# A graph-attention kernel on one core: the score's bias becomes a 17th term of each head, and one VectorE pass sums it

## The chip, the cores and the metric

One core of one Trainium2 chip runs the whole program. The metric is device time in microseconds (us) of one execution, as the median of several. The core has five engines that run side by side and wait for each other through semaphores: TensorE (PE in the profile; its weight loads stand apart as PEld), VectorE (DVE), ScalarE (ACT), GpSimd (POOL) and SyncE (SP), which here only issues DMAs.

## What is computed

The reference is a two-layer graph network over 12,500 nodes and 200,000 edges with vectors of 128 numbers. The change is inside the second layer, an attention over edges with 8 heads of 16 numbers each:

```
scores = einsum('ehd,ehd->eh', q[row], k[col]) / sqrt(16)
scores = scores + edge_emb @ eb_w.T + eb_b          # the bias: 8 numbers per edge
exp_scores = exp(scores - segment_max(scores, row)[row])
attn = exp_scores / segment_sum(exp_scores, row)[row]
out = segment_sum(attn * v[col], row) @ out_w.T + out_b
```

For every edge and head a score is the sum of 16 products of q and k, plus one bias. The division by 4 is already in q, and the 8 biases of every edge were worked out earlier in the kernel.

## The kernel before

The kernel is a sequence of phases with a barrier between them. An earlier phase writes one row per edge into `kv_sorted` in HBM, sorted by the node that collects: 128 numbers of k, then 8 biases (`BIAS_AT` = 128), then a small number `LO_AT` that says which of 128 nodes of a tile the edge belongs to, with v behind them. The score phase reads the first part of these rows (`PART` = 144 numbers).

The score phase works on tiles of 128 edges (an edge per partition). Four tiles are a **group** (`GROUP` = 4), four groups are a **turn** (`GROUPS` = 4), and there are 105 turns, so 420 groups. `by_turns` writes turns 0 and 1 out with fixed numbers and runs nearly all others in a loop of two turns a pass, so an even turn is followed directly by an odd one, and behind an odd one stands the branch back. In the lines below g is the group's number, and j (0 to 3) its place in the turn. What each engine does, in its own order:

- SyncE (`load`, L1873 to L1877) issues one DMA per group, 288 KB into `k_rows`, which holds two turns. It waits until the group two turns earlier has been scored (`scored`) and its `LO_AT` column kept (`lows_kept`).
- TensorE, in `turn`: four matmuls `spread_keys(g + 1)` (L1958), that spread the edges' `LO_AT` over the columns of a bank; then a load of four node numbers from SBUF into registers (`loaded`); then a wait for `hot_ready` and the matmuls of L1991, four of fp32, which the trace records as eight, that pick each edge's q row: bank (2 + j % 2). Behind group 1 of the turn come the three small matmuls of `compare` (L1969 to L1971), behind group 2 the transpose `move_scores` (L1965), and behind group 3 `move_breaks` (L1979), which waits for `flagged`.
- VectorE, in `turn`: `one_hots(g + 1)` (L2019) compares the spread numbers with the partition's own and writes the weights `hot_t`; then `score` of the group before. `score` is two instructions: a TENSOR_REDUCE (L2025) sums the 16 products of each head into `part_scores`, and a TENSOR_TENSOR (L2029) adds the bias from `k_rows` and writes `scores`. At j = 2 `flag` (L2035) follows, on whose `flagged` `move_breaks` waits.
- ScalarE: `lows` (L1889) keeps the `LO_AT` column of a group some two groups ahead, `keep_q(g)` (L1895) copies the q rows from PSUM to `q_sb`; once a turn `keep_scores` (L1899) and `keep_breaks` (L1903).
- GpSimd: one TENSOR_TENSOR (L1946) per group multiplies `q_sb` and the k part of `k_rows` into `qk`, a buffer of two groups; it waits for `q_kept` and for `reduced` of two groups before.

`hot_t`, `q_sb`, `qk`, `part_scores` and the banks are all doubled. All numbers of this path are fp32.

Of the kernel before, what the change touches and what calls it, by code (L numbers as in the profile page):

```python
# [6 lines left out]
ALU, ACT, AX = mybir.AluOpType, mybir.ActivationFunctionType, mybir.AxisListType  # L7

P = 128
N_NODES, N_EDGES, D = 12500, 200000, 128  # L10
HEADS = 8
HEAD_DIM = D // HEADS
# [25 lines left out]
BIAS_AT, LO_AT = D, D + HEADS  # L38
# [15 lines left out]
def need(eng, sem, value):  # L54

    if isinstance(value, int) and value <= 0:
        return
    eng.wait_ge(sem, value)
# [31 lines left out]
def gnn(nc, x, src, dst, attr, w1, b1, w2, b2, gamma, beta, bn_mean, bn_var,  # L90
# [14 lines left out]
    with whole:  # L105
# [98 lines left out]
        with ExitStack() as ph:  # L204
            sem = ph.enter_context(phase_semaphores(nc))
            tmp = lambda n, s, d=F32: ph.enter_context(nc.sbuf_tensor(n, s, d))
# [1389 lines left out]
        with ExitStack() as ph:  # L1596
            own = ph.enter_context(phase_semaphores(nc))
            sem = lambda n: own(f"qkv_{n}")
            tmp = lambda n, s, d=F32: ph.enter_context(nc.sbuf_tensor(f"qkv_{n}", s, d))
# [98 lines left out]
        GROUP = 4  # L1698
        GROUPS = TURN // GROUP


        GROUP = 4
        GROUPS = TURN // GROUP
        with ExitStack() as ph:
            own = ph.enter_context(phase_semaphores(nc))
            sem = lambda n: own(f"expand_{n}")
            tmp = lambda n, s, d=F32: ph.enter_context(nc.sbuf_tensor(f"expand_{n}", s, d))
            spread, hot_ready, made, joined, cleared = (sem(n) for n in ("spread", "hot_ready", "made", "joined", "cleared"))
# [131 lines left out]
        def static_turn(i, *turns):  # L1840

            return isinstance(i, int) and i in turns
# [3 lines left out]
        with ExitStack() as ph:  # L1846
            own = ph.enter_context(phase_semaphores(nc))
            sem = lambda n: own(f"score_{n}")
            tmp = lambda n, s, d=F32: ph.enter_context(nc.sbuf_tensor(f"score_{n}", s, d))
            PIECES = 7  # L1850
            lows_kept, q_in, nodes_placed, shapes, shapes_cleared = (
                sem(n) for n in ("lows_kept", "q_in", "nodes_placed", "shapes", "shapes_cleared"))
            spread, hot_ready, q_ready, q_kept, product, reduced, scored = (
                sem(n) for n in ("spread", "hot_ready", "q_ready", "q_kept", "product", "reduced", "scored"))
            moved, kept_s, differs, flagged, b_moved, kept_b = (
                sem(n) for n in ("moved", "kept_s", "differs", "flagged", "b_moved", "kept_b"))
            k_in = [[sem(f"k_in{b}{j}") for j in range(GROUPS)] for b in range(2)]
            k_rows = tmp("k_rows", [P, 2, GROUPS, GROUP, PART])
            hot_t = tmp("hot_t", [P, 2, GROUP * P])
            q_sb, qk = tmp("q_sb", [P, 2, GROUP * D]), tmp("qk", [P, 2, GROUP * D])  # L1860
            part_scores = tmp("part_scores", [P, 2, GROUP * HEADS])
            scores = tmp("scores", [P, 2, TURN, HEADS])
            flags = tmp("flags", [P, TURN, HEADS], BF16)
            slot_step, tile_step, break_diag = (tmp(n, [P, P], BF16) for n in ("slot_step", "tile_step", "break_diag"))
# [3 lines left out]
            @block.sync  # L1868
            def _(sp):
                q_tiles = q_table.rearrange("(n p) d -> p n d", p=P)  # L1870

                def load(i, b, m):
                    for j in range(GROUPS):  # L1873
                        need(sp, scored, (i - 2) * GROUPS + j + 1)
                        need(sp, lows_kept, (i - 2) * GROUPS + j + 1)
                        rows = kv_turns[:, bass.ds(i, 1), j * GROUP:(j + 1) * GROUP, 0:PART]
                        sp.dma_start(k_rows[:, b, j, :, :], rows.rearrange("p a c f -> p (a c) f")).then_inc(k_in[b][j], 16)  # L1877
                    if static_turn(i, 0):
                        for n in range(PIECES):
                            some = slice(n * NT // PIECES, (n + 1) * NT // PIECES)  # L1880
                            sp.dma_start(nodes[:, some, :], q_tiles[:, some, :]).then_inc(q_in, 16)

                by_turns(sp, load)

            @block.scalar
            def _(act):
                def lows(i, b, m, j):
                    act.wait_ge(k_in[b][j], m * 16 + 16)
                    act.copy(lo_turns[:, bass.ds(i * TURN + TURN + j * GROUP, GROUP)],  # L1889
                             k_rows[:, b, j, :, LO_AT:LO_AT + 1].rearrange("p m a -> p (m a)")).then_inc(lows_kept, 1)  # L1890

                def keep_q(g, b):
                    act.wait_ge(q_ready, g + 1)
                    need(act, product, g - 1)
                    act.copy(q_sb[:, b, :], bank[2 + b][:, :]).then_inc(q_kept, 1)  # L1895

                def keep_scores(i):
                    act.wait_ge(moved, i + 1)
                    act.copy(scores_t[:, bass.ds(i * P, P)], bank[6][:, 0:P]).then_inc(kept_s, 1)  # L1899

                def keep_breaks(i, count):
                    act.wait_ge(b_moved, count)
                    act.copy(breaks[:, bass.ds(i * P, P)], bank[5][:, 0:P]).then_inc(kept_b, 1)  # L1903

                def turn(i, b, m):
                    for j in range(GROUPS):
                        if j < 2:
                            lows(i, b, m, j + 2)
                        elif not static_turn(i, S_TURNS - 1):
                            lows(i + 1, 1 - b, m + b, j - 2)  # L1910
                        keep_q(i * GROUPS + j, j % 2)
                        if j == 3 and not static_turn(i, 0):
                            keep_scores(i - 1)
                        if j == 3 and not static_turn(i, 0, 1):
                            keep_breaks(i - 1, i - 1)

                for j in range(2):
                    lows(0, 0, 0, j)
                by_turns(act, turn)
                keep_scores(S_TURNS - 1)  # L1920
                keep_breaks(S_TURNS - 1, S_TURNS - 1)
                keep_breaks(0, S_TURNS)

            @block.gpsimd
            def _(pool):
                g = nc.gpsimd
                for shape in (slot_step, tile_step, break_diag):
                    g.memset(shape[:, :], 0.0).then_inc(shapes_cleared, 1)
                pool.wait_ge(shapes_cleared, 3)
                g.affine_select(out=slot_step[:, :], in_=slot_step[:, :], compare_op=ALU.not_equal, fill=1.0, base=0,  # L1930
                                pattern=[[-1, P]], channel_multiplier=1).then_inc(shapes_cleared, 1)
                g.affine_select(out=tile_step[:, :], in_=tile_step[:, :], compare_op=ALU.not_equal, fill=-1.0, base=-(P - 1),
                                pattern=[[-1, P]], channel_multiplier=1).then_inc(shapes, 1)
                g.affine_select(out=break_diag[:, :], in_=break_diag[:, :], compare_op=ALU.not_equal, fill=BREAK, base=0,
                                pattern=[[-1, P]], channel_multiplier=1).then_inc(shapes, 1)
                pool.wait_ge(shapes_cleared, 4)
                g.affine_select(out=slot_step[:, :], in_=slot_step[:, :], compare_op=ALU.not_equal, fill=-1.0, base=-1,
                                pattern=[[1, P]], channel_multiplier=-1).then_inc(shapes, 1)

                def turn(i, b, m):  # L1940
                    for j in range(GROUPS):
                        n = i * GROUPS + j
                        pool.wait_ge(k_in[b][j], m * 16 + 16)
                        pool.wait_ge(q_kept, n + 1)
                        need(pool, reduced, n - 1)
                        g.tensor_tensor(qk[:, j % 2, :].rearrange("p (m d) -> p m d", d=D),  # L1946
                                        q_sb[:, j % 2, :].rearrange("p (m d) -> p m d", d=D),
                                        k_rows[:, b, j, :, 0:D], ALU.mult).then_inc(product, 1)

                by_turns(pool, turn)  # L1950

# [61 lines left out]
            def _(dve):  # L2013
                v = nc.vector
# [6 lines left out]
                def score(i, b, j):  # L2021
                    g = i * GROUPS + j
                    dve.wait_ge(product, g + 1)
                    need(dve, scored, g - 1)
                    v.tensor_reduce(part_scores[:, j % 2, :], qk[:, j % 2, :].rearrange("p (m d) -> p m d", d=HEAD_DIM), AX.X, ALU.add).then_inc(reduced, 1)  # L2025
                    dve.wait_ge(reduced, g + 1)
                    if j == 0:
                        need(dve, moved, i - 1)
                    v.tensor_tensor(scores[:, b, j * GROUP:(j + 1) * GROUP, :], k_rows[:, b, j, :, BIAS_AT:BIAS_AT + HEADS],  # L2029
                                    part_scores[:, j % 2, :].rearrange("p (m h) -> p m h", h=HEADS), ALU.add).then_inc(scored, 1)  # L2030

                def flag(count):
                    dve.wait_ge(differs, count)
# [366 lines left out]
```

## Time and profile before

| what | value |
|---|---|
| median of 3 runs | 9340.34 us |
| lowest and highest of them | 9325.51 and 9343.74 us |
| the profiled execution's own time | 9325.89 us |
| its span, first to last instruction | 9324.3 us |
| mean granted TensorE clock over the span | 0.790 |

The profile comes from one execution. A time of the profile is in us from the first instruction. The granted clock is a share of 2.4 GHz. The busy shares of the 40 slices are averages over phases that are bound by different things; the score phase is slices 32 to 36, about 7253 to 8267 us.

### The profile page before, as it was taken

The numbers are of one execution on the slowest core, as the hardware profiler recorded it, in microseconds if no ns is written. First come the engines' busy times: TensorE is split into PE (matmuls) and PEld (weight loads), VectorE is DVE, ScalarE is ACT, GpSimd is POOL, SyncE is SP. The second block draws the span as 40 slices with busy tenths as digits, with TensorE's granted clock in tenths as the row PEclk, the third lists the DMA queues.
The fourth block names the chain that finished last, engine by engine and source line by source line (L and its number), as shares of the span: only waits on it lengthen the run. The fifth ranks groups of instructions, "written<-read, shape, count | busy, mean of one in ns | idle before, by whom it ended". The sixth has DMA issues, their size and how long they took to land. (4 is left out here: it accounts for less than half of the span.)

```text
span 9324.3 us, 229377 instructions
## 1 busy us (share of the span) xinstructions
PE 6847.9 (73%) x40334; PEld 5733.4 (61%) x40335; DVE 6225.0 (67%) x23634; ACT 3314.6 (36%) x10654; POOL 5973.0 (64%) x6648
## 2 busy tenths in 40 slices
PE   7789999999868888888884656666666577735774
PEld 5578888888747777776773444444444466625663
DVE  8755555555547777777776655555555688897777
ACT  7533333333324444444441100000000233316884
POOL 4467776666656666666667577777777455526665
PEclk9876666666668888888885888888888899978997
DMA  1043333333342211111112333333333544414553
GB/s 45 8 113 104 105 104 104 102 102 102 89 124 53 52 51 51 51 50 50 48 49 62 110 113 113 113 113 113 113 113 113 140 126 125 126 51 131 151 153 93
DMA packets 1057790, 868.52 MB, mean 93 GB/s; under 512 B 214825, under 2 KB 950425, under 8 KB 1057737
## 3 DMA queue, kind: packets, MB, share of 16 engines
q0 software_dynamic: 179664, 437.87, 15.4%
q1 hardware_dynamic: 643032, 319.49, 13.1%
q10 hardware_dynamic: 235040, 110.58, 4.2%
q8 instruction: 18, 0.29, 0.0%
q14 instruction: 36, 0.29, 0.0%
HBM read 578.04 MB, written 287.84 MB: 93 GB/s over the span
## 5 line engine op out<-in xcount | busy, mean ns | idle before, releaser
L1420 POOL DMA_INDIRECT spmm_rows<-h_table,spmm_index_ring x3136 | 2968.3, 947 | 1472.4 <-issue 886.2
L1491 PE MATMUL bank<-spmm_rows,spmm_hot 128*128 x6660 | 1951.2, 395 | 117.8 <-SPq L1397 71.1
L1765 POOL DMA_INDIRECT kv_sorted<-expand_payload,expand_where_ring x1568 | 1519.1, 969 | 500.6 <-issue 418.4
L1465 DVE TENSOR_TENSOR region_ab<-region_ab,bank 128x128 f32 x3330 | 956.1, 287 | 1213.9 <-PE bank L1491 1165.9
L1786 PE MATMUL bank<-region_ab,expand_hot_t 128*128 x3336 | 1107.5, 490 | 773.4 <-DVE expand_hot_t L1802 773.1
L1491 PEld LDWEIGHTS bank<-spmm_rows,spmm_hot 128*128 128x128 f32 x6660 | 1421.9, 265 | 214.0 <-issue 184.3
L1818 DVE SCALAR_TENSOR_TENSOR expand_payload<-expand_payload,region_c,bank 128x256 f32 x1668 | 801.5, 481 | 893.7 <-SPq L1730 406.2
L1786 PEld LDWEIGHTS bank<-region_ab,expand_hot_t 128*128 128x128 f32 x3336 | 770.8, 242 | 975.2 <-issue 849.0
L1449 DVE TENSOR_SCALAR spmm_hot<-iota_bf,lo_slots 128x128 f32<-128x128 bf16 x3334 | 1001.3, 300 | 20.0 <-issue 18.7
L1946 POOL TENSOR_TENSOR score_qk<-score_q_sb,score_k_rows 128x512 f32<-128x512 f32 x420 | 532.3, 1267 | 477.4 <-ACT score_q_sb L1895 464.2
L456 ACT ACTIVATE spmm_beside_sign<-iota_half,region_c 128x128 bf16<-128x128 bf16 x1568 | 521.8, 392 | 828.8 <-DVE spmm_beside_bias_sb L545 681.0
L689 PE MATMUL bank<-spmm_beside_next_slot,spmm_beside_lo_t 128*128 128x98 f32 x3136 | 807.3, 346 | 0.3
L1991 PE MATMUL bank<-region_ab,score_hot_t 128*128 x3360 | 521.3, 302 | 211.1 <-ACT score_q_sb L1895 98.4
L2275 PE MATMUL bank<-mix_mixed,mix_hot 128*128 128x136 f32 x3360 | 506.8, 310 | 211.1 <-DVE region_ab L2239 195.0
L724 ACT COPY spmm_beside_next_slot<-bank 128x98 f32<-128x98 f32 x1568 | 379.7, 242 | 744.5 <-PE bank L683 729.2
L2176 POOL TENSOR_TENSOR mix_mixed<-mix_mixed 128x512 f32<-128x512 f32 x420 | 453.4, 1100 | 268.2 <-ACT mix_mixed L2191 178.3
L2275 PEld LDWEIGHTS bank<-mix_mixed,mix_hot 128*128 128x128 f32 x3360 | 466.6, 208 | 249.9 <-DVE region_ab L2239 229.8
L689 PEld LDWEIGHTS bank<-spmm_beside_next_slot,spmm_beside_lo_t 128*128 128x128 f32 x3136 | 580.9, 231 | 49.0
L1991 PEld LDWEIGHTS bank<-region_ab,score_hot_t 128*128 128x128 f32 x3360 | 443.6, 206 | 261.7 <-issue 261.4
L683 PE MATMUL bank<-spmm_beside_hot_hi,spmm_beside_hot_lo 128*128 128x98 bf16 x1568 | 357.7, 228 | 328.2 <-issue 328.2
L1751 ACT COPY expand_where_ring<-region_c 128x8 int32 x196 | 38.7, 197 | 1541.5 <-SPq L1730 1531.1
L469 PE MATMUL bank<-spmm_beside_sign,spmm_beside_hot_hi 128*98 128x128 bf16 x1568 | 453.4, 289 | 162.7 <-ACT spmm_beside_sign L456 76.0
(350 smaller groups left out, 13957.6 us busy)
## 6 DMA issues: line engine op xcount, KB each, us to landing
score_k_rows<-kv_sorted SPq DMA_DIRECT2D x420, 288.0 KB
mix_mixed<-kv_sorted SPq DMA_DIRECT2D x420, 256.0 KB
spmm_beside_attr_sb<-in_edge_attr_dram ACTq DMA_DIRECT2D x390, 256.0 KB
spmm_rows<-h_table,spmm_index_ring POOLq DMA_INDIRECT x3136
kv_sorted<-expand_payload,expand_where_ring POOLq DMA_INDIRECT x1568
kv_sorted<-spmm_beside_blank SPq DMA_DIRECT2D x1, 15232.0 KB
kv_sorted<-spmm_beside_blank SPq DMA_DIRECT2D x98, 136.0 KB
h_table<-region_ab SPq DMA_DIRECT2D x28, 448.0 KB, 3.0
```

The source lines that it names most:

```text
L456: nc.scalar.activation(self.sign[:, slot, :], iota_half[:, :], ACT.Sign, bias=self.lo[:, bass.ds(c, 1)], scale=-1.0).then_inc(self.signs_r ...
L689: t.matmul(self.found_in[k % 2][:, 0:NT], self.lo_t[:, k // 2 % self.PAIRS, at], self.next_slot[:, k % 2, :], start=True, stop=False)
L1420: nc.gpsimd.indirect_dma_start(rows[:, h * HALF + k, :], None, table, bass.IndirectOffsetOnAxis(ap=index_ring[:, h, k:k + 1], axis=0)).the ...
L1449: nc.vector.tensor_scalar(hot[:, k % HOTS, :], iota_bf[:, :], lo_slots[:, bass.ds(t, 1)], None, ALU.is_equal).then_inc(row_hot_ready, 1)
L1465: nc.vector.tensor_tensor(here, here, sum_bank[k % 2][:, 0:D], ALU.add).then_inc(added, 1)
L1491: nc.tensor.matmul(sum_bank[k % 2][:, 0:D], hot[:, k % HOTS, :], tile_of(rows, place[k % HALF]), start=True, stop=True).then_inc(summed, 1)
L1765: nc.gpsimd.indirect_dma_start(kv_sorted, bass.IndirectOffsetOnAxis(ap=where_ring[:, h, k:k + 1], axis=0), payload[:, h * HALF + k, 0:ROW] ...
L1786: nc.tensor.matmul(into, hot_t[:, j % 2, m * P:(m + 1) * P], tile_of(kv_nodes, node[m]), start=True, stop=True).then_inc(made, 1)
L1818: v.scalar_tensor_tensor(here, here, same_window[:, bass.ds(t, 1)], made_here, ALU.mult, ALU.add).then_inc(joined, 1)
L1946: g.tensor_tensor(qk[:, j % 2, :].rearrange("p (m d) -> p m d", d=D), q_sb[:, j % 2, :].rearrange("p (m d) -> p m d", d=D), k_rows[:, b, j ...
L1991: last = nc.tensor.matmul(bank[2 + j % 2][:, n * D:(n + 1) * D], hot_t[:, j % 2, n * P:(n + 1) * P], tile_of(nodes, node[n]), start=True, ...
L2275: last = nc.tensor.matmul(bank[k % RING][:, stream * W:(stream + 1) * W], hot[:, b, c, :], mixed[:, b, c, :], start=True, stop=True)
```

## The change

GpSimd's product writes into a new tile `terms`, in which every head has 17 places in a row, the first 16 for the products. ScalarE gets one more copy per group, `place_bias`, which puts the 8 biases of each edge into the 17th places. VectorE's reduce sums 17 numbers and writes `scores` directly; the TENSOR_TENSOR, `part_scores` and the semaphore `reduced` go. `terms` takes the bytes that `qk` and `part_scores` had together (4,352 per partition). GpSimd waits for `scored` where it waited for `reduced`. SyncE's loads wait for `product` and `bias_placed` where they waited for `scored` and `lows_kept`.

```diff
-            q_sb, qk = tmp("q_sb", [P, 2, GROUP * D]), tmp("qk", [P, 2, GROUP * D])
-            part_scores = tmp("part_scores", [P, 2, GROUP * HEADS])
+            TERMS = HEAD_DIM + 1
+            q_sb, terms = tmp("q_sb", [P, 2, GROUP * D]), tmp("terms", [P, 2, GROUP, HEADS, TERMS])
...
-                        need(sp, scored, (i - 2) * GROUPS + j + 1)
-                        need(sp, lows_kept, (i - 2) * GROUPS + j + 1)
+                        need(sp, product, (i - 2) * GROUPS + j + 1)
+                        need(sp, bias_placed, (i - 2) * GROUPS + j + 1)
...
+                def place_bias(i, b, j):
+                    need(act, scored, i * GROUPS + j - 1)
+                    act.copy(terms[:, j % 2, :, :, HEAD_DIM:TERMS].rearrange("p m h a -> p m (h a)"),
+                             k_rows[:, b, j, :, BIAS_AT:BIAS_AT + HEADS]).then_inc(bias_placed, 1)
...
                         keep_q(i * GROUPS + j, j % 2)
+                        place_bias(i, b, j)
...
-                        need(pool, reduced, n - 1)
-                        g.tensor_tensor(qk[:, j % 2, :].rearrange("p (m d) -> p m d", d=D),
-                                        q_sb[:, j % 2, :].rearrange("p (m d) -> p m d", d=D),
-                                        k_rows[:, b, j, :, 0:D], ALU.mult).then_inc(product, 1)
+                        need(pool, scored, n - 1)
+                        g.tensor_tensor(terms[:, j % 2, :, :, 0:HEAD_DIM],
+                                        q_sb[:, j % 2, :].rearrange("p (m h d) -> p m h d", h=HEADS, d=HEAD_DIM),
+                                        k_rows[:, b, j, :, 0:D].rearrange("p m (h d) -> p m h d", d=HEAD_DIM), ALU.mult).then_inc(product, 1)
...
                     dve.wait_ge(product, g + 1)
-                    need(dve, scored, g - 1)
-                    v.tensor_reduce(part_scores[:, j % 2, :], qk[:, j % 2, :].rearrange("p (m d) -> p m d", d=HEAD_DIM), AX.X, ALU.add).then_inc(reduced, 1)
-                    dve.wait_ge(reduced, g + 1)
+                    dve.wait_ge(bias_placed, g + 1)
                     if j == 0:
                         need(dve, moved, i - 1)
-                    v.tensor_tensor(scores[:, b, j * GROUP:(j + 1) * GROUP, :], k_rows[:, b, j, :, BIAS_AT:BIAS_AT + HEADS],
-                                    part_scores[:, j % 2, :].rearrange("p (m h) -> p m h", h=HEADS), ALU.add).then_inc(scored, 1)
+                    v.tensor_reduce(scores[:, b, j * GROUP:(j + 1) * GROUP, :].rearrange("p m h -> p (m h)"),
+                                    terms[:, j % 2, :, :, :].rearrange("p m h d -> p (m h) d"), AX.X, ALU.add).then_inc(scored, 1)
```

## Rows read from the trace of the kernel before

**Rows 1.** TensorE's busy tenths and granted clock in 40 slices of the span

```profile
PE   7789999999868888888884656666666577735774
...
PEclk9876666666668888888885888888888899978997
```

**Rows 2.** Groups of instructions in the score phase: busy us, mean ns | idle before, releaser

```profile
L1946 POOL TENSOR_TENSOR score_qk<-score_q_sb,score_k_rows 128x512 f32<-128x512 f32 x420 | 532.3, 1267 | 477.4 <-ACT score_q_sb L1895 464.2 <-DVE score_part_scores L2025 13.1
...
L2019 DVE TENSOR_SCALAR score_hot_t<-bank,iota_p 128x512 f32<-128x512 f32 x420 | 311.7, 742 | 52.2 <-PE bank L1958 48.5
L2025 DVE TENSOR_REDUCE score_part_scores<-score_qk 128x32 f32<-128x512 f32 x420 | 283.4, 675 | 94.3 <-POOL score_qk L1946 94.3
L2029 DVE TENSOR_TENSOR score_scores<-score_k_rows,score_part_scores 128x32 f32<-128x32 f32 x420 | 276.2, 658 | 14.4
```

**Rows 3.** The tile part_scores: durations in ns, min/median/max, of its two instructions

```profile
L2025 DVE TENSOR_REDUCE score_part_scores<-score_qk x420: 668/672/689, 7287.2 to 8265.0; 128x32 f32<-128x512 f32 x140
L2029 DVE TENSOR_TENSOR score_scores<-score_k_rows,score_part_scores x420: 191/781/1272, 7287.9 to 8265.7; 128x32 f32<-128x32 f32 x140
```

**Rows 4.** Line L1991 alone in one stretch: us, PE busy (count), PEld, PEclk, DMA share, GB/s

```profile
7300.00:8256.00 956.00, 506.02 (x3264) 430.49 (x3264) 0.95 0.50 126
```

**Rows 5.** VectorE and GpSimd in order of time: start us, us, instruction

```profile
7541.02 0.94 DVE L2029 TENSOR_TENSOR score_scores<-score_k_rows,score_part_scores 128x32 f32<-128x32 f32 x1
7541.89 0.28 DVE L2035 TENSOR_SCALAR score_flags<-bank 128x128 bf16<-128x128 f32 x1
...
7540.65 1.26 POOL L1946 TENSOR_TENSOR score_qk<-score_q_sb,score_k_rows 128x512 f32<-128x512 f32 x1 [0.97 <-ACT score_q_sb L1895]
```

**Rows 6.** TensorE in order of time, an odd turn (from 7534.67) between two even ones

```profile
7532.19 1.15 PE L1991 MATMUL bank<-region_ab,score_hot_t 128*128 x8 [0.92 <-DVE score_hot_t L2019]
...
7534.67 1.16 PE L1991 MATMUL bank<-region_ab,score_hot_t 128*128 x8 [0.59 <-issue]
...
7536.56 1.16 PE L1991 MATMUL bank<-region_ab,score_hot_t 128*128 x8 [0.51 <-ACT score_q_sb L1895]
...
7538.80 1.15 PE L1991 MATMUL bank<-region_ab,score_hot_t 128*128 x8 [0.51 <-ACT score_q_sb L1895]
...
7540.83 1.15 PE L1991 MATMUL bank<-region_ab,score_hot_t 128*128 x8 [0.54 <-ACT score_q_sb L1895]
7542.22 0.23 PE L1979 MATMUL bank<-score_break_diag,score_flags 128*128 128x128 bf16 x1 [0.23 <-DVE score_flags L2035]
...
7544.16 1.15 PE L1991 MATMUL bank<-region_ab,score_hot_t 128*128 x8 [0.60 <-issue]
...
7546.06 1.15 PE L1991 MATMUL bank<-region_ab,score_hot_t 128*128 x8 [0.52 <-ACT score_q_sb L1895]
...
7548.43 1.15 PE L1991 MATMUL bank<-region_ab,score_hot_t 128*128 x8 [0.51 <-issue]
...
7550.52 1.16 PE L1991 MATMUL bank<-region_ab,score_hot_t 128*128 x8 [0.52 <-ACT score_q_sb L1895]
...
7553.39 1.15 PE L1991 MATMUL bank<-region_ab,score_hot_t 128*128 x8 [0.59 <-issue]
```

**Rows 7.** TensorE in order of time, an odd turn that starts at half clock

```profile
7703.30 2.07 PE L1991 MATMUL bank<-region_ab,score_hot_t 128*128 x8 [0.62 <-issue]
...
7705.59 1.52 PE L1991 MATMUL bank<-region_ab,score_hot_t 128*128 x8
...
7707.45 1.16 PE L1991 MATMUL bank<-region_ab,score_hot_t 128*128 x8
...
7709.94 1.15 PE L1991 MATMUL bank<-region_ab,score_hot_t 128*128 x8 [1.00 <-DVE score_hot_t L2019]
...
7712.82 0.93 PE L1991 MATMUL bank<-region_ab,score_hot_t 128*128 x6 [0.64 <-issue]
```

**Rows 8.** Groups of instructions of the whole program, as in group 2

```profile
L1754 ACT COPY expand_payload<-expand_bias_ring 128x64 f32<-128x64 f32 x196 | 47.9, 244 | 351.2 <-DMA expand_bias_ring<-bias_tab 351.2
...
L2082 POOL TENSOR_TENSOR region_ab<-region_ab 128x3360 f32<-128x3360 f32 x1 | 17.7, 17726 | 139.9 <-DVE region_ab L2118 139.9
```

More of the change, by code:

```diff
@@ L1852, in gnn @@
                 sem(n) for n in ("lows_kept", "q_in", "nodes_placed", "shapes", "shapes_cleared"))
-            spread, hot_ready, q_ready, q_kept, product, reduced, scored = (
-                sem(n) for n in ("spread", "hot_ready", "q_ready", "q_kept", "product", "reduced", "scored"))
+            spread, hot_ready, q_ready, q_kept, product, bias_placed, scored = (
+                sem(n) for n in ("spread", "hot_ready", "q_ready", "q_kept", "product", "bias_placed", "scored"))
             moved, kept_s, differs, flagged, b_moved, kept_b = (
```

## The prediction

> **What bounds the kernel now.** I read the page first, for TensorE's two rows of slices [rows 1]: the change touches only the score phase, and the rest I leave as it is. Then the groups of that phase [rows 2], to see which engine has the work; the tile's own view [rows 3], to see whether a duration is a price or a wait; one line in one stretch [rows 4], for the period; and last the engines in order of time [rows 5 to 7], because only there can be seen who waits for whom.
>
> The period: between 7300 and 8256 us there are 3,264 records of L1991, 32 to a turn, so 102 turns in 956 us: 9.373 us a turn, 2.34 a group [rows 4]. Per group VectorE is busy 742 + 675 + 658 ns [rows 2], four times 2.075, and 0.28 for the flag [rows 5]: 8.58 us of a turn's 9.37. It looks like the bound, and GpSimd with 1.267 of 2.34 does not.
>
> The third of the three durations isn't a price. The TENSOR_TENSOR of L2029 handles 32 numbers per partition, yet takes between 191 and 1272 ns, while the reduce before it, on 512 numbers, always takes 668 to 689 [rows 3]. The rows in time show what it is: L2029 runs from 7541.02 to 7541.96, GpSimd's product from 7540.65 to 7541.91 [rows 5]. It ends some 50 ns behind the product, and the longest one is as long as a whole product. I read it as an instruction with two SBUF inputs that can't go on while GpSimd's product runs; 191 ns is its price alone.
>
> Is VectorE then the bound? TensorE must be asked, since it closes each period. I take the distance from one start of L1991 to the next. An odd turn goes 1.89, 2.24, 2.03, 3.33 us (from 7534.67 to 7544.16); the next even one 1.90, 2.37, 2.09, 2.87 (to 7553.39) [rows 6]. In the short three nobody waits for VectorE: TensorE has four spreading matmuls, a register load of half a microsecond (the idle time of 0.51 to 0.60 before L1991, whatever name stands behind it), and 1.15 us of matmuls. In the fourth there is a real wait, L1979 on the flag (0.23 us idle, then the queue starts up again), since the flag at 7541.89 stood behind the stretched L2029 [rows 5, 6]. So the two engines are nearly equal, and **VectorE costs TensorE only the lateness at the end of a turn**, not its whole surplus.
>
> How long is the fourth distance with no wait? An even turn shows it: 7532.19 to 7534.67 is 2.48, with no idle time named at L1979. An odd turn shows 7709.94 to 7712.82, 2.88: the loop's branch is in that one [rows 6, 7].
>
> **The change, part by part.**
>
> *Removed: L2029 and the waits beside it*, 420 instructions, 276 us of VectorE [rows 2]. *Grown: the reduce*, from 512 to 544 numbers. Row L2025 gives 1.31 ns a number with its fixed part inside [rows 3], so at most 0.042 us more; at the least nothing. I take 0.035. VectorE's turn falls from 8.58 to 4 x (0.742 + 0.675 + 0.035) + 0.28 = 6.1 us, far below TensorE's.
>
> *Added: ScalarE's copy*, 32 numbers. The nearest row copies 64 from SBUF to scattered places in 0.244 us [rows 8], so between nothing and 0.244; I take 0.22, or 0.9 us a turn. It stands behind the copy of q, for which GpSimd waits, so it delays no product of its own group, and the reduce needs it only when the product of 1.267 us is done. Its wait for `scored` of two groups earlier could hold ScalarE, and with it `lows` and the next `keep_q`. That score is queued on VectorE directly behind the one-hots that L1991 of this very group needed, so it is over some 0.7 us after L1991 began, while ScalarE gets to the copy only after L1991's 1.15 us and its own 0.6. Cost: nothing; without this cover ScalarE would pay the difference per group.
>
> *Moved: where the product writes.* The inputs are the same, but the output goes in runs of 16 with a gap of one. No row of before has such an output on GpSimd. From below 1.267 us [rows 2]; nothing makes it cheaper. From above, the dearest product per number in the trace, 17.7 us for 3,360 numbers or 5.28 ns, makes 2.70 us for 512 [rows 8]. That one ran alongside VectorE's own subtraction; the shape is nearest to L1946 itself, so I take 1.27. Up to about 2.2 us per group, TensorE's period, it stays hidden.
>
> *Moved: SyncE's waits.* The loads wait for the product and the bias copy, both earlier than the score. ScalarE keeps the lows of a group before its bias, so dropping that wait changes nothing. DMA is busy 0.50 of the stretch and the loads run a turn ahead [rows 4]; worth nothing in either direction. GpSimd now waits for the whole score of two groups before, which is the reduce it always waited for.
>
> *What is late next.* The product of a group starts 1.85 us behind its L1991 (7538.80 to 7540.65) [rows 5, 6] and ends at 3.1; the reduce of 0.71 ends at about 3.9. The flag, queued behind the score of group 1, is then done 4.2 us after group 1's L1991 began. L1979 asks for it after two more distances and 1.15 us of matmuls, 2.24 + 2.03 + 1.15 = 5.4 at the earliest. The one-hots of a group start at the latest 2.0 us after the L1991 two groups before theirs (3.9 less a distance of 1.89), end at 2.8, and are wanted at 4.1. Both have over a microsecond to spare, so all waits of TensorE for VectorE should go, and TensorE's own issue and matmuls set the turn.
>
> *The sum.* Without waits an even turn is 1.90 + 2.37 + 2.09 + 2.48 = 8.84 us, an odd one 1.89 + 2.24 + 2.03 + 2.88 = 9.04, mean 8.94. Against 9.373 that is 0.433 a turn, 102 turns: 44 us. Some distances could still hold a little waiting that I can't see; if even turns issued as quickly as odd ones (2.24 and 2.03 for 2.37 and 2.09) it would be 0.53 a turn, 54 us. The first turns and the phase's tail lose one stretched L2029 or two: 1 us. So **45 us less**. In terms of the profiled execution 9325.9 becomes 9281; that one stands at the low end of the runs shown, and the median of 9340.3 is what is compared, so it becomes 9295.
>
> **Rivals.**
>
> *The stretch passes on, or had no hold on the end: no change, 9340.* If whatever GpSimd holds falls on the next VectorE instruction, the reduce would now take up to 1.27 us and the flag be as late as before. Against it: reduces that overlapped products throughout never exceeded 689 ns [rows 3]. The Trainium skill ("VectorE: DVE Perf Modes", The TRN2 errata) gives an fp32 tensor_tensor (N + 151)/0.96 ns, which is 191 for N = 32. By that rule VectorE's turn would be 6.7 us, never late, and the change would be worth nothing; the trace agrees with the smallest duration only, and has a mean of 658. Both together 0.10.
>
> *Half the gain: 9318.* One of the margins above is eaten, by the added semaphore waits or by a product that costs 1.5 us or more, and the flag is late in one of the two turns of a pass: 51 times 0.4 to 0.5 us less than forecast. Nothing shows it, only estimates exclude it. 0.13.
>
> *TensorE's clock falls: slower.* The granted clock is 0.95 in this stretch [rows 4], and 0.6 in slices in which TensorE is busy 9 tenths and more, 0.8 in those with 8 [rows 1]. If a fuller TensorE brought it to 1.2 GHz (half clock) more often, L1991 takes 2.07 us instead of 1.15 and the distance behind it 2.29 instead of 1.89 [rows 7]: 0.40 a group, 4 a turn. It eats 45 us once a quarter to 30% of the 408 groups go at 1.2 GHz; now about a tenth does. At a share of one half the time is 9295 + 0.4 x 408 x 0.40 = 9360. Against it: the half-clock stretches stand right behind the turn's long last distance, 3.33 or 2.87, where TensorE had idled longest, and now that distance shrinks; and the half-clock turn's first two distances add to 4.15, against 4.13 at 2.4 GHz [rows 6, 7], since the register load overlaps the slower matmuls. The Trainium skill ("TensorE: Matmul & The Clock Gate", Part 1) has it that idling lowers the clock and activity releases it; by that rule the half-clock stretches would rather vanish and the sum be 9293. 0.05.
>
> *GpSimd becomes the bound: slower.* At the upper price of 2.70 us a group the phase takes 420 x (2.70 - 2.34) = 151 us more, 9491; it turns against the change above 2.34. 0.02.
>
> **How the numbers follow.** The forecast 9295 has 0.70, its own range 9280 to 9308: the two sums of 44 and 54 us and the runs' spread. The rivals have 0.10, 0.13, 0.05 and 0.02. The range of eight in ten runs from 9275 to 9325, which takes in the half gain. Faster by over 0.2% means below 9321.7, about what a measurement of this kernel can tell from no change: the forecast and two thirds of the half gain, 0.79. Within 0.2%: the no-change rival and the rest, 0.14. Slower: 0.07.
>
> **What the changed profile would show.** VectorE's reduce at 0.70 to 0.71 us, never longer, and no idle time at L1979 on the flag nor at L1991 on the one-hots. Distances of L1991 of about 1.9, 2.3, 2.05 and then 2.5 or 2.9. The product at 1.27, ScalarE's new copy at 0.20 to 0.24 with no idle time before it. The turn at 8.9 us. It would be wrong if reduces stretch, if the product is over 2.2 us, if the clock falls under 0.85 in this stretch, or if one of the three short distances grows.

## The result, and the profile after

The changed kernel takes 9243.0 us (median of 4 runs, 9235.72 to 9259.46) against 9341.32 us before (median of 4, 9325.51 to 9343.74): ratio 0.9901, 95% interval 0.9883 to 0.9918, so 77 to 109 us less. The forecast was 9295, 45 us less, with a range from 9275. The direction was right and the gain was twice what I worked out.

The profiled execution took 9239.79 us, 86.1 less than that of before. The page of the changed kernel, its head and TensorE's two rows of slices:

```profile
span 9238.2 us, 229276 instructions
...
PE   7789999999958888888886556666666577736773
...
PEclk9876666666668888888886787887888899978997
```

The phases before the change are where they were: the first L1991 (now L1997) starts at 7283.03 us, and at 7283.02 before. The groups of the score phase, which answer to [rows 2] (busy us, mean ns, idle before and releaser):

```profile
L1952 POOL TENSOR_TENSOR score_terms<-score_q_sb,score_k_rows 128x512 f32<-128x512 f32 x420 | 533.7, 1271 | 389.7 <-ACT score_q_sb L1900 369.6 <-DVE score_scores L2033 19.9 <-issue 0.2
...
L2025 DVE TENSOR_SCALAR score_hot_t<-bank,iota_p 128x512 f32<-128x512 f32 x420 | 312.8, 745 | 35.1 <-PE bank L1964 26.8
L2033 DVE TENSOR_REDUCE score_scores<-score_terms 128x32 f32<-128x544 f32 x420 | 302.4, 720 | 275.0 <-POOL score_terms L1952 274.8
...
L1894 ACT COPY score_terms<-score_k_rows 128x32 f32<-128x32 f32 x420 | 104.2, 248 | 0.0
```

The product with its gaps costs 1.271 us (1.267 before), ScalarE's copy 0.248 with no idle time ahead of it, the reduce 0.720 at the mean. VectorE now idles 275 us waiting for products, so it has slack. L1997 alone in the same 102 turns as in [rows 4] (us, PE busy, PEld busy, granted clock, DMA share, GB/s):

```profile
7297.77:8170.59 872.82, 470.56 (x3264) 394.88 (x3264) 1.00 0.53 137
```

8.557 us a turn in place of 9.373: 0.816 less, 83.2 us in 102 turns. The first two turns give 2.3 us more, the last turn and the tail about 1. Where in the turn does it come from? TensorE in order of time, an even turn and the odd one behind it, which answer to [rows 6]:

```profile
7555.16 1.15 PE L1997 MATMUL bank<-region_ab,score_hot_t 128*128 x8 [0.60 <-issue]
...
7557.05 1.15 PE L1997 MATMUL bank<-region_ab,score_hot_t 128*128 x8 [0.51 <-ACT score_q_sb L1900]
...
7559.41 1.15 PE L1997 MATMUL bank<-region_ab,score_hot_t 128*128 x8 [0.52 <-issue]
...
7561.51 1.15 PE L1997 MATMUL bank<-region_ab,score_hot_t 128*128 x8 [0.51 <-ACT score_q_sb L1900]
7562.50 0.22 PE L1985 MATMUL bank<-score_break_diag,score_flags 128*128 128x128 bf16 x1
7562.56 0.45 PE L1964 MATMUL bank<-ident_bf,lo_turns 128*128 128x128 bf16 x4
7563.63 1.15 PE L1997 MATMUL bank<-region_ab,score_hot_t 128*128 x8 [0.62 <-ACT score_q_sb L1900]
...
7565.51 1.15 PE L1997 MATMUL bank<-region_ab,score_hot_t 128*128 x8 [0.50 <-ACT score_q_sb L1900]
...
7567.76 1.15 PE L1997 MATMUL bank<-region_ab,score_hot_t 128*128 x8 [0.54 <-ACT score_q_sb L1900]
...
7569.75 1.15 PE L1997 MATMUL bank<-region_ab,score_hot_t 128*128 x8 [0.50 <-ACT score_q_sb L1900]
```

The reader is to see three distances that did not move at all, 1.89, 2.36, 2.10 and 1.88, 2.25, 1.99, as forecast, and a fourth of 2.12 us in the even turn (7561.51 to 7563.63). In the odd one it is 2.52 (the next start is 7572.27). I had forecast 2.48 and 2.88. Nearly the whole miss is 0.36 us in one place of each turn.

What was wrong with 2.48 can be seen in the two kernels' rows around the flag's matmul. VectorE before: the flag of the even turn that I had taken as free of a wait, that of the next even turn, and that of the odd turn that I had taken as free (its last L1991 starts at 7709.94 [rows 7]):

```profile
7532.77 0.28 DVE L2035 TENSOR_SCALAR score_flags<-bank 128x128 bf16<-128x128 f32 x1
...
7551.52 0.28 DVE L2035 TENSOR_SCALAR score_flags<-bank 128x128 bf16<-128x128 f32 x1
...
7710.54 0.28 DVE L2035 TENSOR_SCALAR score_flags<-bank 128x128 bf16<-128x128 f32 x1
```

and TensorE before, at the first of them:

```profile
7533.18 0.22 PE L1979 MATMUL bank<-score_break_diag,score_flags 128*128 128x128 bf16 x1
7533.46 0.61 PE L1958 MATMUL bank<-ident_bf,lo_turns 128*128 128x128 bf16 x4
```

The flag ended at 7533.05, while the last L1991's matmuls, begun at 7532.19 [rows 6], ran until 7533.34. So no matmul idled, and yet the next of the four spreading matmuls (`spread_keys`) came 0.28 us behind L1979, where in the changed kernel it comes 0.06 behind (7562.50 to 7562.56), and its four matmuls are done in 0.45 instead of 0.61 us. The hypothesis that the runs had to test: TensorE's issue reaches the wait for the flag long before the array does, and while it stands there it prepares nothing of what follows.

The trace has records of TensorE's sequencer too, its waits and register instructions, which the rows shown leave out. In all 102 turns of both kernels the instruction just ahead of the flag's wait is over 0.48 to 0.51 us after the turn's last big matmul group began. In the kernel before, the sequencer's next record begins 0.05 us behind the end of the flag, in all 102 turns. In the changed kernel it begins 0.13 us after the start of the one ahead of it, again in all 102. So in the kernel before the sequencer stood at the flag from about 0.49 us on, while the matmuls ran to 1.15.

### The profile page after: what moved, and what is told of

It reads as the page before. It is cut to its first block and busy times, and to the rows that moved or that the text cites. A ratio compares the mean times of both kernels' runs of the same rounds, so it can differ in the third digit from the quotient of the medians.

```text
span 9238.2 us, 229276 instructions
## 1 busy us (share of the span) xinstructions
PE 6786.1 (73%) x40334; PEld 5668.8 (61%) x40335; DVE 5985.6 (65%) x23214; ACT 3366.2 (36%) x11074; POOL 5983.4 (65%) x6648
## 5 line engine op out<-in xcount | busy, mean ns | idle before, releaser
L1952 POOL TENSOR_TENSOR score_terms<-score_q_sb,score_k_rows 128x512 f32<-128x512 f32 x420 | 533.7, 1271 | 389.7 <-ACT score_q_sb L1900 369.6
L1997 PE MATMUL bank<-region_ab,score_hot_t 128*128 x3360 | 486.2, 288 | 222.0 <-ACT score_q_sb L1900 164.8
L1997 PEld LDWEIGHTS bank<-region_ab,score_hot_t 128*128 128x128 f32 x3360 | 408.4, 192 | 278.9 <-issue 278.8
```

The source lines that it names most:

```text
L1952: g.tensor_tensor(terms[:, j % 2, :, :, 0:HEAD_DIM], q_sb[:, j % 2, :].rearrange("p (m h d) -> p m h d", h=HEADS, d=HEAD_DIM), k_rows[:, b ...
L1997: last = nc.tensor.matmul(bank[2 + j % 2][:, n * D:(n + 1) * D], hot_t[:, j % 2, n * P:(n + 1) * P], tile_of(nodes, node[n]), start=True, ...
```

## The experiments

Three readings stood against each other. **A**: the late flag holds TensorE's issue, also where no matmul idles, and this is the whole gain. **B**: the one-hots behind the flag were what was late. **C**: part of the gain is the clock, since its granted share rose from 0.95 to 1.00 in this stretch.

**before_flag_first.** The kernel before, with one statement moved in VectorE's order.

```diff
                             one_hots(i * GROUPS + j + 1, (j + 1) % 2)
+                        if j == 2 and not static_turn(i, 0, 1):
+                            flag(i - 1)
                         if j > 0:
                             score(i, b, j - 1)
                         elif not static_turn(i, 0):
                             score(i - 1, 1 - b, GROUPS - 1)
-                        if j == 2 and not static_turn(i, 0, 1):
-                            flag(i - 1)
```

> The kernel before, with one thing moved: at j = 2 VectorE computes the flag before that group's score, not behind it. L2029 stays and still stretches. Theory A (the late flag holds TensorE's issue: everything behind move_breaks waits until the flag is there, also where no matmul idles): the fourth distance of L1991 falls to 2.1 us in even turns and 2.5 in odd ones, the turn to 8.6 to 8.9 us, the time to 9250 to 9290. Theory B (the one-hots of the next group are what is late; they stand behind the same L2029): the fourth distance stays above 2.8 and the time above 9320. Theory C (half of the gain came from the clock, whose half-speed stretches vanished): at most half the gain, 9290 or more, with the fourth distance at 2.5 and 2.9.

Measured: 9252.18 us against 9335.38, ratio 0.9909 (0.9892 to 0.9925), so 83 us less without any part of the change. Its 102 turns, and its VectorE group of L2029:

```profile
7304.58:8179.35 874.77, 473.42 (x3264) 397.72 (x3264) 1.00 0.54 137
```

```profile
L2029 DVE TENSOR_TENSOR score_scores<-score_k_rows,score_part_scores 128x32 f32<-128x32 f32 x420 | 301.5, 718 | 14.4
```

8.576 us a turn, with L2029 still there and longer than before (0.718 us at the mean against 0.658). Theory A stands, B falls: the one-hots were as much behind L2029 as before. Of the 83.2 us that the change takes off the 102 turns, this one statement takes 81.3.

Reading C is not settled by this run, since the clock is at 1.00 here as well. The turns of the kernel before settle it. In 26 of its 102 turns a part went at half clock, and the granted clock over the turn was 0.84 or less. Those took 9.29 us (even) and 9.56 us (odd) at the mean, the others 9.24 and 9.50 (without the last turn), so all their half clock cost under 2 us. The turns at full clock alone became 0.8 us shorter.

**after_flag_mid and after_flag_late.** The changed kernel, with the flag made late in two doses: moved to j = 3 in front of the score and behind the next one-hots; and there with a reduce of 512 constants ahead of it.

```diff
-                        if j == 2 and not static_turn(i, 0, 1):
-                            flag(i - 1)
+                        if j == 3 and not static_turn(i, 0, 1):      # in front of score(); both kernels
+                            need(dve, spared, i - 2)                 # these two lines: after_flag_late alone
+                            v.tensor_reduce(spare[:, :], ident[:, :].unsqueeze(1).to_broadcast([P, GROUP, P]), AX.X, ALU.add).then_inc(spared, 1)
+                            flag(i - 1)
```

> The changed kernel with the flag moved behind the next group's one-hots (j = 3). It then ends about 0.5 us after the start of the turn's last L1997, 0.9 later than now, and 0.6 before that group's matmuls are through. Theory A puts the point from which it costs at about 0.5: fourth distance 2.1 to 2.2 and 2.5 to 2.6, time within 10 us of 9243. The reckoning of the prediction (a wait costs only once the matmuls are through): no change.

> As the one before, plus one VectorE reduce of 0.67 us on constants in front of the flag, which then ends about 1.1 us after the last L1997 began, still before its matmuls are through (1.15). Theory A: the fourth distance is the flag's end plus 1.6 us in even turns, plus 2.0 in odd ones, so 2.7 and 3.1; 0.6 us a turn, time about 9300, with hardly any idle time at the matmul that waits for the flag. The prediction's reckoning: the wait is hidden by the matmuls, time 9243 to 9250.

Measured: 9251.93 us for the first, ratio 0.9921 (0.9904 to 0.9937) to the kernel before; 9348.46 us for the second, ratio 1.0024 (1.0014 to 1.0034). TensorE and the flag in after_flag_late, an even turn:

```profile
7477.19 1.15 PE L1998 MATMUL bank<-region_ab,score_hot_t 128*128 x8 [0.51 <-ACT score_q_sb L1901]
7478.32 0.23 PE L1986 MATMUL bank<-score_break_diag,score_flags 128*128 128x128 bf16 x1
...
7479.87 1.15 PE L1998 MATMUL bank<-region_ab,score_hot_t 128*128 x8 [0.62 <-issue]
```

```profile
7477.98 0.28 DVE L2040 TENSOR_SCALAR score_flags<-bank 128x128 bf16<-128x128 f32 x1
```

The flag is there at 7478.26, 1.07 us after the start of L1998 and just before its matmuls end at 7478.34. No idle time stands at L1986, and the distance is 2.68 instead of 2.12. The table puts the cases together: the end of the flag, counted from the start of the turn's last big matmul group, and the fourth distance, which starts with that group, in one turn each:

| kernel | turn | flag's end | fourth distance | difference |
|---|---|---|---|---|
| changed | even | -0.39 | 2.12 | |
| before_flag_first | even | -0.44 | 2.11 | |
| after_flag_mid | even | 0.47 | 2.13 | 1.66 |
| before | even (7532.19) | 0.86 | 2.48 | 1.62 |
| after_flag_late | even | 1.07 | 2.68 | 1.61 |
| before | even (7550.52) | 1.28 | 2.87 | 1.59 |
| after_flag_mid | odd | 0.49 | 2.50 | 2.01 |
| after_flag_late | odd | 1.09 | 3.09 | 2.00 |
| before | odd (7540.83) | 1.34 | 3.33 | 1.99 |

Earlier than about 0.5 us after the start the flag costs nothing; later than that, every 0.1 us costs 0.1. Over half a microsecond of that lies under running matmuls. The turns of the table are no choice of good cases: in the kernel before and in after_flag_late, 99 of 102 turns have a fourth distance within 0.05 us of the flag's end plus 1.60 (even) or 2.00 (odd). In the changed kernel all 51 even turns, with the flag early, lie between 2.09 and 2.17.

The law held; my total for after_flag_late, 9300, did not. In 53 turns the flag ended at 1.05 to 1.1 us, and they took 9.14 us at the mean; 102 such turns would have made 9300. In the other 49 a part of the turn went at half clock (the stretch below has 0.91), the flag ended only at 1.5 to 2.0 us, and they took 9.93 us at the mean. That VectorE, with the added reduce, had less room to catch up in them is my reading and was not tested.

```profile
7299.09:8269.95 970.86, 534.86 (x3264) 455.80 (x3264) 0.91 0.48 124
```

**after_two_input, after_one_input, after_one_source.** What stretches a short VectorE instruction? The changed kernel with one more of them behind each reduce, on constants, with an output that nobody reads, in three kinds.

```diff
+                    need(dve, spared, g - 1)
+                    v.tensor_tensor(spare[:, j % 2, :], ident[:, 0:32], ident[:, 32:64], ALU.add).then_inc(spared, 1)   # after_two_input
+                    v.tensor_reduce(spare[:, j % 2, :], ident[:, 0:64].rearrange("p (a b) -> p a b", b=2), AX.X, ALU.add).then_inc(spared, 1)   # after_one_input
+                    v.tensor_scalar(spare[:, j % 2, :], ident[:, 0:32], 1.0, None, ALU.add).then_inc(spared, 1)   # after_one_source
```

> The changed kernel plus one VectorE TENSOR_TENSOR of 32 numbers behind each reduce, with two constant SBUF inputs and an output nobody reads. If an instruction with two SBUF inputs can't go on during GpSimd's product, it takes 0.19 to 1.27 us, mean 0.6, as L2029 did, the flag is late again, and the turn is 9.2 to 9.4 us, the time 9310 to 9340. If L2029's length came from its own data (reading k_rows, waiting for the reduce), it takes 0.19 and the time stays at 9243 to 9250.

> The changed kernel plus one VectorE TENSOR_REDUCE of 64 constant numbers to 32 behind each reduce, so a short instruction with one SBUF input in the same place. Port theory: 0.2 us each time, VectorE's turn is 0.8 us longer, the flag still early, the time 9243 within 5. Rival (any further VectorE instruction costs the same): as slow as the two-input one.

> The changed kernel plus one VectorE TENSOR_SCALAR, 32 constant fp32 numbers from SBUF to SBUF, behind each reduce. If only two SBUF inputs make VectorE wait for GpSimd: 0.1 to 0.2 us each, time 9243 to 9260. If a one-input instruction from SBUF to SBUF takes the same port while it runs: stretched to about 0.6 on the mean, time 9310 to 9340.

The added instruction in the three kernels, in this order (its durations in ns, min/median/max):

```profile
L2037 DVE TENSOR_TENSOR score_spare<-ident x420: 173/697/1231, 7297.1 to 8273.3; 128x32 f32<-128x32 f32 x140
```

```profile
L2037 DVE TENSOR_REDUCE score_spare<-ident x420: 206/209/211, 7309.7 to 8201.6; 128x32 f32<-128x64 f32 x140
```

```profile
L2037 DVE TENSOR_SCALAR score_spare<-ident x420: 160/704/1210, 7293.6 to 8269.7; 128x32 f32<-128x32 f32 x140
```

Times: 9336.79 us (ratio 1.0002, 0.9992 to 1.0011), 9257.68 (0.9912, 0.9896 to 0.9929) and 9332.77 (0.9998, 0.9988 to 1.0008). The two-input instruction on constants, far from `k_rows`, brings the whole old time back, with a turn of 9.369 us. So L2029's length had nothing to do with its data. The reduce with one input costs 0.209 us each time, and the turn stays at 8.558 us. Its median is 15 us above that of the changed kernel, where I had expected at most 5; but of the 28 us between the two profiled executions 22 lie ahead of the score phase (its first L1997 starts at 7304.96 us and not at 7283.03). The third kind I had left open: an instruction with one tensor input (TENSOR_SCALAR), from SBUF to SBUF in fp32, waits just like the two-input one. The Trainium skill ("GPSIMD Engine Reference", Specifications) speaks of "contention with DVE instructions in a 2-port perf mode or with two SBUF inputs", and the Trainium skill ("VectorE: DVE Perf Modes", The perf-mode tier table) lists the fp32 tensor_scalar in SBUF at twice the base rate and the reduce at the base rate. The trace agrees in which of the three kinds waited: medians of 0.697 and 0.704 us against 0.209.

**before_bias_copy.** The kernel before plus the change's ScalarE copy alone, with its waits on ScalarE, VectorE and SyncE.

```diff
+                def place_bias(i, b, j):
+                    need(act, scored, i * GROUPS + j - 1)
+                    act.copy(spare[:, j % 2, :, :, HEAD_DIM:HEAD_DIM + 1].rearrange("p m h a -> p m (h a)"),
+                             k_rows[:, b, j, :, BIAS_AT:BIAS_AT + HEADS]).then_inc(placed, 1)
...
                         keep_q(i * GROUPS + j, j % 2)
+                        place_bias(i, b, j)
```

> The kernel before plus the change's ScalarE copy alone, into a tile nobody reads, with the same waits (ScalarE's for scored, VectorE's and SyncE's for the copy). Prediction's reckoning: hidden, 0.25 us each with no idle time, time within 10 us of the kernel before. Rival: the added waits on VectorE or ScalarE cost, 20 us or more.

Measured: 9337.0 us against 9331.76, ratio 1.000 (0.9991 to 1.001), the copy 0.248 us with no idle time ahead of it. It is hidden, as the prediction had it, and the added waits cost nothing that can be told from the spread of the runs.

**after_load16 and after_load8.** If TensorE's own issue sets the turn now, its register loads are the next thing to cut. The changed kernel, with the node numbers of a turn, or of two groups, loaded at once:

```diff
-                        node = loaded(mybir.EngineType.PE, node_at[0:1, bass.ds(i * TURN + j * GROUP, GROUP)], GROUP, NT - 1, CLAMPED)
+                        if j % 2 == 0:                                                   # after_load8
+                            two = loaded(mybir.EngineType.PE, node_at[0:1, bass.ds(i * TURN + j * GROUP, 2 * GROUP)], 2 * GROUP, NT - 1, CLAMPED)
+                        node = two[j % 2 * GROUP:(j % 2 + 1) * GROUP]
```

> The changed kernel, but TensorE loads the 16 node numbers of a turn into registers at once instead of 4 per group. If TensorE's issue sets the turn, three of four loads with their 0.5 us of idle matmuls go: 1.0 to 1.5 us a turn, the time 9090 to 9140, less if VectorE or GpSimd now becomes late. If something else sets it: within 10 us of 9243.

> The changed kernel, but TensorE loads 8 node numbers every other group. The load of 16 took 1.11 us and that of 4 takes 0.34 in the traces, so one of 8 should take 0.6 and two of them 1.2 against 1.36, and two register set-ups less of about 0.15 us: 0.4 us a turn less, time near 9200, if no stretch becomes long enough to bring the half clock back. With the half clock back as in the kernel with one load a turn: 9240 to 9260.

The load of 16 missed: 9252.47 us (ratio 0.9906, 0.9889 to 0.9922), no better than the changed kernel. At full clock three distances did fall, in odd turns to 1.38, 1.72 and 1.74 us, but the load made one long gap at the end of the turn. In 42 of the 102 turns a part went at half clock, as right behind this gap:

```profile
7564.68 0.22 PE L1985 MATMUL bank<-score_break_diag,score_flags 128*128 128x128 bf16 x1
7566.38 0.65 PE L1964 MATMUL bank<-ident_bf,lo_turns 128*128 128x128 bf16 x4 [1.48 <-ACT lo_turns L1889]
7567.13 2.07 PE L1998 MATMUL bank<-region_ab,score_hot_t 128*128 x8
```

(The name behind 1.48 is the profile's guess at a releaser; by the sequencer's records the load is in the gap.) The turns at full clock took 7.90 us (even) and 8.29 (odd), the 42 others 9.16 at the mean. The load of 8 gave 9186.29 us (ratio 0.984, 0.9824 to 0.9857), 57 us below the changed kernel and 145 below the one before: the best of all. Its windows, first that of after_load16 and then that of after_load8:

```profile
7310.93:8181.96 871.03, 518.91 (x3264) 444.80 (x3264) 0.92 0.55 138
```

```profile
7295.33:8117.66 822.33, 470.72 (x3264) 394.95 (x3264) 1.00 0.58 146
```

8.062 us a turn at full clock, against 8.540 at 0.92. By the sequencer's records a load takes 0.334 us for 4 numbers, 0.590 for 8 and 1.107 for 16. With loads of 8, the distances that lost their load are 0.50 us shorter and those with the longer load 0.26 us longer.

**before_first_load8 and after_load8_again.** Is VectorE's removed work worth anything of its own? The kernel before with the flag first and loads of 8 (the two diffs above together), beside the changed kernel with loads of 8.

> The kernel before with the flag first and TensorE's loads of 8 node numbers, so L2029 stays with its stretch. With the flag first alone the turn was 8.58 us, with TensorE as the bound. TensorE's own turn is now 8.06 us. If VectorE's removed work is worth something once TensorE is that fast, VectorE holds it: it has 0.742 + 0.672 + 0.2 to 0.72 us a group and a flag, 6.7 to 8.8 us a turn, so turn 8.3 to 8.6, time 9220 to 9255, against 9186 of the changed kernel with the same loads. Rival (only the flag's place ever mattered; L2029's stretch shrinks as the schedule tightens): the turn is 8.06 and the time 9186 to 9200.

> The changed kernel with loads of 8 again, for the comparison on the same chip: 9186 within 10, turn 8.06 us.

This pair ran on a chip on which the phases ahead of this one take 3.2 ms longer (the kernel before: 12503.11 us), with a granted clock of 0.66 in them against 0.76. So it is compared within itself, and of what was expected only the turns can be held against it: 12403.2 and 12372.83 us, ratios to the kernel before 0.9923 (0.9909 to 0.9936) and 0.9898 (0.9883 to 0.9913). The score phase is the same there, as the second kernel's window shows beside that of the other chip:

```profile
10462.88:11312.82 849.94, 473.22 (x3264) 397.53 (x3264) 1.00 0.56 141
```

```profile
10475.15:11297.60 822.45, 470.56 (x3264) 394.88 (x3264) 1.00 0.58 146
```

8.333 us a turn against 8.063: 27.5 us in 102 turns, of the 30 between the medians. In this stretch TensorE's big matmul groups waited 201 times for the one-hots in the first kernel, 146.9 us in all; in the second none of their waits is put down to the one-hots. Once TensorE needs only 8.06 us a turn, VectorE's stretched L2029, ahead of the one-hots, holds it a little. So the change is worth some 28 us more than the reordering there, and 2 us of the phase's turns (8.576 against 8.557) in the kernel as it was.

## Why the prediction was half right

*What bounds.* Right: TensorE sets three of four distances, VectorE only delays the end of a turn through the flag. L2029's duration is a wait for GpSimd's product, and the rival that another instruction would inherit it did not come true; the reduce goes up to 722 ns.

*The parts.* The copy costs 0.248 us where I took 0.22, the product 1.271 for 1.27, the reduce 0.720 for 0.710, and all are hidden as I said. The flag is done 4.07 us after group 1's L1997 began (7557.05 to 7561.12), where I had 4.2.

*The step that failed* is "How long is the fourth distance with no wait?", with "no idle time named at L1979" as its evidence: the sum put 2.48 and 2.88 us where the runs showed 2.12 and 2.52. No idle time at the matmul was no evidence that the wait was free. The same error stands in "What is late next", where I let L1979 ask for the flag only when the matmuls ahead of it were through, 1.15 us after their start; the issue asks at about 0.5. The two turns I took as free of waiting had the flag at 0.86 and 0.88 us and paid about 0.36. Both had begun with a stretch at half clock; in most turns of the kernel before the flag came at 1.26 to 1.39. The term should have been 8.557 a turn in place of 8.94, which over 102 turns makes 39 us. With the first two turns and the tail, 2 us more than I allowed, that gives the 86 between the two profiled executions: 45 plus 41. The medians lie 98 apart; the rest is within what they scatter (77 to 109).

*The upper sum* of 54 us let even turns issue as fast as odd ones; they did not (2.36 and 2.25 as before). *The clock rival* was wrong in sign here: the half-clock stretches vanished with the long distances, as the rule of the Trainium skill ("TensorE: Matmul & The Clock Gate", Part 1) had it; the trace agrees, 1.00 after 0.95. They were next to no part of the gain either: under 2 us, as worked out above, because the half-clock turns of the kernel before were hardly longer than its others. Where no late flag covers them they do cost: 8.94 us for 8.49 in two even turns of before_flag_first, and 8.9 to 9.4 for 7.9 to 8.3 in all but the last of the 42 of after_load16. One reading of [rows 1] was too smooth: two of the slices with 8 tenths have 0.7 and 0.6 of the clock, and not 0.8. The sum does not use it.

Even and odd turns differ by 0.11 us in the second and third distance, though nobody waits there. In the changed kernel the sequencer has one instruction more in each of these distances of an even turn, in all 51 (17 against 16, and 15 against 14), and one such step takes about 0.1 us. Why the program has it there stays open.

## What to carry to other kernels

A wait of TensorE was paid at its issue here, not at its array. To ask whether one is free, compare the releaser's end with the moment at which the instruction ahead of the waiting one was issued, and look at how closely the instructions behind it follow. A short VectorE instruction whose duration scatters up to the length of a GpSimd one may be waiting for it, as L2029 was. Small signals that another engine needs then belong ahead of it in the queue: moving one statement gave 83 of the 98 us. And when the issue is the bound, it can pay to spread what stalls it: loads of 8 gave 57 us, and the load of 16, with its one long gap and the half clock behind many of them, nothing.

## What the runs showed of the hardware that was not expected

- TensorE was held by a semaphore that came 0.3 us before its matmuls ran out. Its sequencer stood at the wait from 0.49 us after the start of the 1.15 us of matmuls, and went on 0.05 us after the flag.
- A VectorE TENSOR_SCALAR of 32 fp32 numbers from SBUF to SBUF, with a single tensor input, took up to 1.21 us beside a GpSimd product of 1.27 us (median 0.704), while a TENSOR_REDUCE in the same place took 0.206 to 0.211.
- Two loads of 8 registers made the turn 0.495 us shorter than four of 4 (8.062 against 8.557), and one of 16 gave nearly all of that back (8.540), with a gap of 1.48 us a turn and half clock in 42 of 102 turns.
